# Attention block with feed-forward on one core: weights split sooner, tile 4's reciprocal sooner, the early output product moved into the next head, and the last head's turned probabilities made on TensorE

## The reference

```
h   = layernorm(x) * (1 + ca) + sa
q,k = rope(h @ wq), rope(h @ wk)        # 32 heads, 8 key/value heads, width 128
att = softmax(mask(q @ k.T / sqrt(128)))
x   = x + ga * (concat(att @ v) @ wo)
h   = layernorm(x) * (1 + cb) + sb
x   = x + gb * (h @ W.T + b + low_rank(h, rank picked by a router))
```

## Time and profile before

| what | value |
|---|---|
| device time, 3 runs | 1119.62, 1121.52 (median), 1125.44 us |
| the profiled execution: its time, its span in the trace | 1124.94 us, 1123.2 us |
| PE busy | 1058.5 us (94%) |
| PEld busy | 870.2 us (77%) |
| DVE busy | 778.5 us (69%) |
| ACT busy | 638.1 us (57%) |
| POOL busy | 522.2 us (46%) |
| granted TensorE clock, mean | 0.990 |

### The profile page before, as it was taken

One profiled execution on the slowest core, in us unless ns is written; L12 is line 12 of the kernel. 1 busy time (PEld: TensorE's weight loads), 2 busy tenths in 40 slices (PEclk: granted clock), 3 DMA queues, 4 the chain that ended last, 5 costly groups with the idle time before them and its releaser, 6 DMA issues.

```text
span 1123.2 us, 16527 instructions
## 1 busy us (share of the span) xinstructions
PE 1058.5 (94%) x5416; PEld 870.2 (77%) x5416; DVE 778.5 (69%) x1834; ACT 638.1 (57%) x1298; POOL 522.2 (46%) x506
## 2 busy tenths in 40 slices
PE   6999989998999999998999989999999989998998
PEld 3668878887888878886888868887788878886775
DVE  4668865688558865688557865678647875678476
ACT  5547764477347764477337754477536754477343
POOL 2535553366325553365334643456425653455144
PEclk8999999999999999999999999999999999999899
DMA  6462322123302323123202223033212223033001
GB/s 210 149 216 67 108 72 76 49 83 94 90 5 67 108 71 76 51 81 95 70 25 66 85 76 93 10 96 106 53 58 67 76 88 92 10 96 121 11 20 57
DMA packets 99005, 88.22 MB, mean 79 GB/s; under 512 B 39461, under 2 KB 84645, under 8 KB 98793
## 3 DMA queue, kind: packets, MB, share of 16 engines
q1 hardware_dynamic: 98920, 87.17, 26.2%
HBM read 59.88 MB, written 27.26 MB: 78 GB/s over the span
## 4 chain that ended last, share of the span: by engine, by line
PE 59%; DVE 13%; ACT 11%; POOL 7%; issue 6%; DMA 4%; SPq 1%; POOLq 0%; DVEq 0%; ACTq 0%
PE accumulators L650 15%; PE accumulators L680 13%; PE accumulators L665 12%; PE scores L610 9%; PE transposed L623 6%; DVE p_large L1173 3%; POOL qc L1546 3%; DVE turned L1197 2%; ACT pa_hi L914 2%; ACT p_large L900 2%; POOL qr L1542 2%; DMA stage<-in_L_attn_wv_dram 2%; ACT qr L933 2%; PE scores L865 2%; ACT qr L932 2%
## 5 line engine op out<-in xcount | busy, mean ns | idle before, releaser
L908 ACT ACTIVATE pb_hi<-transposed 128x512 fp32r<-128x512 f32 (+3 forms) x256 | 120.8, 511 | 203.9 <-PE transposed L623 203.7
L1533 POOL TENSOR_SCALAR p_large<-p_large,rowinv 128x640 f32<-128x640 f32 (+3 forms) x128 | 125.1, 978 | 236.3 <-DVE rowinv L1178 236.2
L1542 POOL TENSOR_TENSOR qr<-qr,trig 128x512 f32<-128x512 f32 x80 | 104.4, 1306 | 221.3 <-ACT qr L933 221.3
L1185 DVE TENSOR_TENSOR pb_lo<-transposed,pb_hi 128x512 fp32r<-128x512 f32 (+3 forms) x256 | 141.9, 585 | 78.6 <-ACT pb_hi L908 78.2
L900 ACT ACTIVATE p_large<-p_large,negmax 128x640 f32<-128x640 f32 (+3 forms) x128 | 126.2, 986 | 97.9 <-DVE negmax L1173 96.9
L610 PE MATMUL scores<-k_hi,q_hi 128*128 128x512 f32 (+2 forms) x384 | 139.5, 363 | 1.7 <-DVE negmax L1173 1.7
L1173 DVE CUSTOM_DVE_ANT_0 p_large<-scores,mask 128x640 f32<-128x640 f32 (+3 forms) x128 | 129.7, 1013 | 16.2 <-PE scores L610 13.2
L610 PE MATMUL scores<-k_hi,q_lo 128*128 128x512 f32 (+2 forms) x384 | 131.5, 343 | 0.0
L610 PE MATMUL scores<-k_lo,q_hi 128*128 128x512 f32 (+2 forms) x384 | 131.1, 341 | 0.0
L1533 POOL TENSOR_SCALAR p_small<-p_small,rowinv 128x128 f32<-128x128 f32 (+3 forms) x128 | 97.2, 774 | 71.6 <-DVE rowinv L1178 71.6
L623 PE MATMUL transposed<-ident,p_large 128*128 128x128 f32 x832 | 114.6, 276 | 14.0 <-POOL p_large L1533 14.0
(11 more groups left out here) (165 smaller groups left out, 2228.7 us busy)
## 6 DMA issues: line engine op xcount, KB each, us to landing
p_rows<-turned SPq DMA_DIRECT2D x32, 640.0 KB, 2.9
pa_lo<-p_rows SPq DMA_DIRECT2D x128, 160.0 KB, 3.2
stage<-in_L_attn_wq_dram SPq DMA_DIRECT2D x32, 256.0 KB, 2.8
stage<-in_L_attn_wo_dram SPq DMA_DIRECT2D x32, 256.0 KB, 2.7
v_rows<-vt SPq DMA_DIRECT2D x32, 128.0 KB, 2.2
v_lo<-v_rows SPq DMA_DIRECT2D x32, 128.0 KB, 3.2
y<-in_L_wmod_dram SPq DMA_DIRECT2D x4, 512.0 KB, 6.1
stage<-in_L_attn_wk_dram SPq DMA_DIRECT2D x8, 256.0 KB, 2.7
```

Source lines behind the costliest of these rows:

```text
L908: nc.scalar.activation(pt_of(i, part, True), src, ACT.Copy).then_inc(t_hi, 1)
L1185: nc.vector.tensor_tensor(pt_of(i, part, False), src, f32(pt_of(i, part, True)), ALU.subtract).then_inc(t_lo, 1)
L1533: nc.gpsimd.tensor_scalar(row(i), row(i), rowinv[:, i:i + 1], 1.0, ALU.mult, ALU.mult).then_inc(s_norm, 1)
L1542: nc.gpsimd.tensor_tensor(qr[:, s, :], qr[:, s, :], trig[:, 1, half * HALF:(half + 1) * HALF], ALU.mult).then_inc(r_sin, 1)
```

## The change

What it does, part by part:

- `pva` of a head is no longer run at the end of its own `back`, but in the next head's `front`, between score tile 2 and the transposes of tile 7. ACT takes `output_hi` and the tile 7 copies after the exponentials of tiles 0 and 1; DVE takes `output_lo` and the tile 7 subtractions after the mask of tile 2 and the first two reciprocals.
- In heads 1 to 3 DVE makes tile 4's reciprocal ahead of tile 5's mask.
- In head 3 the split of the next group's key weight stands right behind tile 4's exponential (ACT) and tile 5's mask (DVE); the split of `wo 3` and its scaling on POOL stand at the end of the head. The load of the value weight goes ahead of that of `wo 3`, and ahead of the early rows' DMAs of head 3.
- In head 0, DVE takes out the first `wo` product ahead of tile 7's reciprocal, and ACT makes `early_hi` behind tile 7's exponential.
- In the tail the last head's early rows are not turned through DRAM: PE transposes them (four banks `e 0` to `e 3` with 4, 3, 2, 1 blocks), ACT and DVE split each. The feed-forward weight transposes and `wo 0` stand in another order.

The diff, cut:

```
@@ DMA queue, per group
                 if g:
-                    load(("v", 0), at)
+                    load(("wo", 3), at, -1)
                     load(("q", 1), at)
...
                     load(("q", 0), at, 1)
                     load(("k", 0), at, 1)
-                    load(("wo", 3), at)
+                    load(("v", 0), at, 1)
...
-                turn_columns(R * g + 3)
+                if g + 1 < GROUPS:
+                    turn_columns(R * g + 3)
@@ PE, front and back
                 scores(h, 2, at)
                 if h or not at.first:
+                    weighted(hb, 0, at, ahead)
                     transposes(hb, 7, at, ahead)
...
                 transposes(h, 6, at)
-                weighted(h, 0, at)
@@ PE, tail
             scores(3, 4, G7)
+            early_transposes(0)
+            early_transposes(1)
+            scores(3, 5, G7)
             pe.wait_ge(f_in, 16)
             weight_transposes(0)
-            scores(3, 5, G7)
+            early_transposes(2)
+            early_transposes(3)
             weight_transposes(1)
+            weighted(3, 0, G7)
             transposes(3, 4, G7)
             scores(3, 6, G7)
+            weight_transposes(2)
             transposes(3, 5, G7)
-            weight_transposes(2)
+            weight_transposes(3)
             scores(3, 7, G7)
-            weight_transposes(3)
-            weighted(3, 0, G7)
-            transposes(3, 6, G7)
...
+            project_out(0, G7, 0)
...
-            project_out(0, G7, 0)
+            transposes(3, 6, G7)
             project_out(1, G7, 0)
@@ ACT, front and back
+                fill(h, 1, at)
+                exp(h, 0, at)
+                exp(h, 1, at)
                 if h or not at.first:
                     output_hi(hb, 0, at, ahead)
-                fill(h, 1, at)
-                if h or not at.first:
                     transposed_hi(hb, 7, at, ahead)
-                exp(h, 0, at)
-                exp(h, 1, at)
                 exp(h, 2, at)
...
                 exp(h, 4, at)
+                if last:
+                    split_hi(("k", 0), at, 1)
                 exp(h, 5, at)
...
-                if last:
-                    split_hi(("k", 0), at, 1)
-                    split_hi(("wo", 3), at)
                 exp(h, 6, at)
...
-                early_hi(h, at)
+                if h:
+                    early_hi(h, at)
...
                 exp(h, 7, at)
+                if not h:
+                    early_hi(h, at)
...
                 transposed_hi(h, 6, at)
+                if last:
+                    split_hi(("wo", 3), at)
@@ DVE, front and back
+                fill(h, 1, at)
+                masked(h, 2, at)
+                inverse(h, 0, at)
+                inverse(h, 1, at)
                 if h or not at.first:
                     output_lo(hb, 0, at, ahead)
-                fill(h, 1, at)
-                masked(h, 2, at)
-                if h or not at.first:
                     transposed_lo(hb, 7, at, ahead)
                 masked(h, 3, at)
-                for i in range(3):
-                    inverse(h, i, at)
+                inverse(h, 2, at)
...
                 fill(h, 2, at)
+                if h:
+                    inverse(h, 4, at)
                 masked(h, 5, at)
-                inverse(h, 4, at)
+                if not h:
+                    inverse(h, 4, at)
+                if last:
+                    split_lo(("k", 0), at, 1)
...
+                adds = fillers(h, 5, at.first)[:-1] if not h else []
+                fill(h, 5, at, slice(0, min(1, len(adds))))
                 inverse(h, 7, at)
...
+                if last:
+                    split_lo(("wo", 3), at)
@@ the new split of the last head's early rows
+            def early_row_hi(j):
+                act.wait_ge(t_full, N.value("t", ("e", j), G7))
+                nc.scalar.activation(pa_row(pa_hi, j), row_bank(j), ACT.Copy).then_inc(t_hi, 1)
...
+            def early_row_lo(j):
+                dve.wait_ge(t_hi, N.value("t", ("e", j), G7))
+                nc.vector.tensor_tensor(pa_row(pa_lo, j), row_bank(j), f32(pa_row(pa_hi, j)), ALU.subtract).then_inc(t_lo, 1)
```

More of the change, by code:

```diff
@@ L149, in front @@
         if before[1] >= 0:
+            self.job(("pva", before[0], 0), before[1])
             self.banks(before[0], 7, before[1])
@@ L170, in back @@
         self.banks(h, 6, g)
-        self.job(("pva", h, 0), g)
     def tail(self):
@@ L624, in transposes, with early_transposes @@
                     mm.then_inc(t_full, 1)
+            def early_transposes(j):
+                name = ("e", j)
+                need(pe, s_norm, N.value("s", (3, 3), G7))
+                b = N.slot("t", name, G7)
+                need(pe, t_lo, back_of(N.value("t", name, G7), 2))
+                for i in range(j, 4):
+                    mm = nc.tensor.transpose(TB[:, b, (i - j) * P:(i - j + 1) * P], row(i)[:, j * P:(j + 1) * P], ident[:])
+                mm.then_inc(t_full, 1)
             def bank_free(name, at, ahead):
@@ L639, in weighted @@
                     pe.wait_ge(v_lo_done, at.g + ahead + 1)
-                    steps = [(pa_hi_done, n, hi_lo[:2], range(4)), (pa_lo_done, n, hi_lo[2:], range(4))]
+                    steps = [(t_lo, N.value("t", ("e", 3), at, ahead), hi_lo, range(4))] if n > LAST else [(pa_hi_done, n, hi_lo[:2], range(4)), (pa_lo_done, n, hi_lo[2:], range(4))]
                 else:
```

78 lines of the change are left out of this document (46 added, 32 removed).

## The result

| | before | after |
|---|---|---|
| device time, median of 15 runs | 1122.97 us (1119.62 to 1130.35) | 1117.15 us (1112.13 to 1123.86) |
| ratio of the runs | | 0.9944, 95% interval 0.9924 to 0.9964 |
| the profiled execution: time, span | 1124.94, 1123.2 us | 1113.62, 1111.8 us |
| granted TensorE clock of the profiled execution | 0.990 | 0.993 |
| POOL busy | 522.2 us | 503.6 us |

The changed kernel is 0.56% faster, a gain of 5.8 us. 1110 was forecast, 13 us or 1.2% under the median before as now known: less than half of the forecast gain came. The time lies inside the full range (1094 to 1124), but just outside 1104 to 1116, the range of the forecast's own case. In a second series, with the changed kernel sent in again, the ratio was 0.9917 (0.9888 to 0.9946), so the best estimate lies between 0.991 and 0.995.

A forecast was written before the change was run, and what follows sets the result against it. PE, busy 94% of the span, bounds the kernel. Seven ordinary groups −4.9, late value weight and half clock −7.3, group 0 +2.05, tail −5.0: together −15.2 from 1124.94, so 1110 us; range 1094 to 1124.

The forecast's parts named there:

- the forecast's own case: Whole kernel: the summed terms hold and give 1110 us, own range 1104 to 1116; chance 0.50.
- Tile 4's reciprocal: Heads 1 to 3: PE's stall before tile 4's transposes goes, tile 5's wait some 0.2; net 0.45 us per head.
- The wait before `pvb`: ACT's exponentials delay `pvb` by 1.1 us: head 2 +0.5, head 3 +1.55, heads 0 and 1 taken as 0.
- rival B: The wait at `pvb` is in every head, heads 0 and 1 too: +17, 1127 us; chance 0.15.
- rival A: The wait at `pvb` is hidden, heads 2 and 3 gain 0.45 each: 23.6 less, 1087 us; chance 0.13.
- The boundary: Between groups: waits for `wk_lo` (0.84) and part of the values' bank (0.5) go, plus head 3's 0.45: −1.8 us.
- The tail with group 7: Tail: no DMA in the chain, `pva` and tile 7's transposes start sooner, −5.0 us (bounds −2 to −7.7).
- Late value weight and half clock gone: −7.3: Two slow group periods, each 3.65 us longer with a late value weight and half clock, become ordinary: −7.3 us.
- are read only by `pva`: Turned rows land later behind the value weight's load, harmless since their reader `pva` moved 4 to 6 us later.
- C: The new waits halve PE's clock once a group: 13 us more, 1123 us; chance 0.07.
- D: Tail or boundary doesn't do what it says, waits move or the values' bank stays late: 1116 us; chance 0.15.
- POOL's neighbour: POOL's addition beside DVE's shifted work: the shared-interface rule would win some 5 us; taken as 0.

The follow-up runs named there:

- the better one: Kernel before, with only the keys' swap (ACT) and `times_cos` (DVE) moved ahead of the value weight's split in head 3: 1114.16 us, ratio 0.9916.

## Why the prediction was right and wrong

By profile against profile, the sum of its terms was 15.2 and 11.4 of the span were measured; by the medians 5.8 (or 8.8 in the second series) were measured. Point by point, "forecast" with the prediction's terms:

- **Tile 4's reciprocal**: right. The wait before tile 4 is gone, a small one before tile 5 (0.25) and tile 6 came; alone it gives 0.9 a group, not 1.35.
- **The wait before `pvb`**: right in place and cause, and in what it costs the heads. The waits themselves, 1.52 and 1.68 by the starts, are not the "about 1" and "2" forecast, but head 2 lasts 0.50 longer and head 3 1.53 longer than before, forecast +0.5 and +1.55. With the old order all of it is gone. Heads 0 and 1 kept their cover, so rival B is out; rival A is out as well (its sum, 1110 − 23.6, is 1086). That POOL's scaling and ACT's split carry head 3's part is borne out by the 0.54 that is left without them in group 2, and not in the two groups where the wait stayed.
- **The boundary**: from head 3's late product to the values −1.56, forecast −1.8. The values' wait fell to 1.5 to 1.6 in ordinary groups, as forecast. The ordinary group fell by 0.94, forecast 0.7; 0.4 more than counted came in heads 0 and 1.
- **The tail with group 7**: −3.45, forecast −3.9 (−5.0, and +1.1 for the group's heads). `pva` waits 1.33, by the trace for `pa_lo`, forecast 1.75 for a bank. The second wait, 1.62, is not the forecast 2.0 of the first output projection for its bank (that one is 0.34) but the low-rank weights' transposes waiting for a DMA, where the prediction had none in the chain. About 1.7 of the 3.45 is a shorter stretch of half clock: the 20 us from 1027 to 1047 of before have a mean clock of 0.83, those from 1024 to 1044 of after 0.91. In the two profiles this is made up again by a stretch in group 0, 0.89 from 55 to 70 us after and 1.00 before.
- **What failed is the term of the sum "Late value weight and half clock gone: −7.3", and with it the sentence that the turned rows may land later since they "are read only by `pva`".** The value weight is no longer late, but the six periods behind the first together fell by 8.1, where six ordinary gains of 0.94 make 5.6: only 2.5 of the 7.3 came. The turned rows took its place. SP now issues their DMAs behind the value weight's load, and ACT copies them (`early_hi`) ahead of exponential 7 and of the keys' swap, so that it is ACT, not PE, that waits for them. ACT's waits before (two lines) and after (one), and its timeline after, ahead of the values' wait of 2.00:

```profile
ACT wv_hi L962 <- DMA stage<-in_L_attn_wv_dram: 10.3, 7, 2.6
...
ACT pa_hi L914 <- DMA pa_lo<-p_rows: 1.1, 2, 0.7
```

```profile
ACT pa_hi L943 <- DMA pa_lo<-p_rows: 6.9, 9, 1.8
```

```profile
651.94 1.28 ACT L943 ACTIVATE pa_hi<-pa_lo 128x1280 fp32r<-128x1280 f32 x1 [0.85 <-DMA pa_lo<-p_rows]
```

Before, PE's idle time ahead of the values was ACT's wait for the value weight plus 0.86 to 0.89, at all seven boundaries. After, it is ACT's wait for the turned rows (0.31 to 0.85) plus 1.13 to 1.17 at six of them, and 1.30 at the one where the rows are in time. At the end of head 1 of groups 4 and 6 ACT waits 1.39 and 1.82 for rows, and from head 1's late product to head 2's it takes 24.63 and 25.02 there, not 23.27. An estimate from these times: 2.3 us at the boundaries (above 1.30 each) and 3.6 at the ends of head 1, some 6 us in all, where 4.8 is missing. At the boundary the order of the loads is the cause: with the boundary of before in the changed kernel ACT waits there for the value weight again and never for rows. In head 1 it is not the loads alone, since in the kernel before with only the reciprocal moved ACT waits for rows there too, up to 1.28.
- **The half clock in that term** was one profiled execution's, and what stays of the waits still draws it: none at the boundaries of the first profile after, two in the second of the same kernel. I had read that the median of before lay 3.4 below the profile and still subtracted the term in full; without it the sum is 1122.97 − 7.9 = 1115, beside 1117.15 and 1115.67 measured. That 1115 comes so near is partly luck: the gain in heads 0 and 1 came out larger than forecast, those of the boundary and the tail smaller.
- **Rivals C and D**: the time lies near D's 1116, but not by its mechanism, since the boundary and the tail gave most of what was counted for them; only at two boundaries did the values' wait stay at 1.96 and 2.00. C was partly true, at another place than I put it. The clock does not fall behind the new waits of 1.5 to 1.7 before `pvb` (in no profile) but behind the old one before the values. The Trainium skill ("TensorE: Matmul & The Clock Gate", HAM oscillation — how this bites in real kernels) tells of waits that bring the clock down again at every turn of a loop; the traces agree for this wait, once per group at most, and show that the same wait does it in one execution and not in another.
- **POOL's neighbour**: by the rows I took 0, and that was right for the addition, which still takes 1.63 in head 1. POOL's busy time fell by 18.6 us all the same: the normalising of the early rows by 22.8 and the additions by 2.7, while the scaling of `wo` rose by 6.5. No wait of PE names these rows.

What stays open: which of the stretches the unprofiled runs hold; why the weights and rows land latest at the boundaries around 530 and 660 us in most of the kernels; and why the reciprocal alone draws more half clock than the kernel before, with waits hardly longer.

## What to carry to other kernels

A product moved within an engine's list costs nothing by itself; what counts is what the engines that feed its successors must now finish first, and this chain could be priced from the trace of before (3.00 forecast, 3.03 measured). When a wait for one DMA is taken away, look for the next DMA that the same engine meets ahead of the same step, and at every reader of what will now land later, not only at the last one. A stretch of half clock that one profiled execution shows is a draw: charge it at what the median of the runs holds, and ask whether the wait in front of it is gone or only shorter. And compare edits by medians: the fastest run of one kernel had the profile that made two kernels look equal. Of the two edits tried alone on the kernel before, the better one took a bank out ahead of long instructions whose results were needed later.

## What the runs showed of the hardware

The same wait of 2.0 to 2.3 us before a product was followed by half clock in 6 of 21 cases, in the same code too (2.11 with, 2.12 without); up to 1.9 in none of 35, from 3.2 on in all 6. A stretch of 3.4 at half clock costs about 1.7 us, an estimate: half of its length, PE being busy in it (rows of the second profile). The subtraction for the queries on DVE, 0.69 in the mean, took 1.70 beside a POOL multiplication with two tensors from SBUF, which itself kept its 1.27. POOL's normalising of the first early tile (128x128) fell from 0.66 to 0.37 in the mean: in three of four heads of before it stood beside that same subtraction (0.74 to 0.77), after beside subtractions that read a PSUM bank, or beside none (0.37). Which two instructions stand side by side was here worth a factor of two to two and a half to one of them.
